# First layer norm in two halves, the attention's constants written during it, and its output in a buffer that is free again

## The chip, the cores and the metric

The kernel runs on one core of one Trainium2 chip. The metric is the device time of one execution in microseconds (us); lower is better. Four compute engines and the DMA queues run their own instruction streams, and semaphores order them against each other.

## The reference, cut to what matters

All tensors are float32, T = 128 x 32 = 4096 tokens of width D = 128. Two stages follow each other, each adding to `x`:

```python
x = x + _L0_ffn_ref(_L0_cond_ref(x, fside, cond), ...)      # Sinkhorn scaling, then a routed FFN
x = x + _L1_ffn_ref(_L1_cond_ref(x, cond, ...), ...)        # a GRU over 32 steps, then the block below
# _L1_ffn_ref:
m = mean(y); v = mean(square(y - m)); n1 = (y - m) * rsqrt(v + 1e-5) * ln1_w + ln1_b
y = y + msa(n1)                     # 16 heads of width 8, 32 tokens of each batch attend to each other
y = y + moe(layernorm(y, ln2_w, ln2_b))     # argmax over 8 experts, gelu, hidden width 512
```

The change touches the first layer norm of `_L1_ffn_ref` and the start of its attention.

## The kernel before, in words

The program is a row of blocks. A block gives every engine a piece of straight code, and the next block begins when all engines have left it. In order: `sinkhorn`, `plan_ffn_gru`, `norm_first`, `attend_and_route`, `experts`. There is no planner: within a block each engine executes its instructions in the order written, and a wait holds everything behind it on that engine.

The GRU leaves its output `ys` with the feature in the partition (`buf_a`). `norm_first` works on N = 32 tiles of 128 tokens, in CHUNKS = 8 chunks of TC = 4 tiles.

- **Turning.** TensorE multiplies each tile of `ys` with `turn_gate` (L864: an identity and eight gate columns), which puts tokens in the partitions. ScalarE copies each chunk from PSUM into `rows` (L894). There are two PSUM buffers `ps_n`.
- **Statistics.** VectorE takes mean and variance of every tile with `bn_stats` (L935), four for each chunk, in a hardware loop. After the eighth chunk it combines them for all 32 tiles at once: seven small operations in `variance` (L809 to L815), each waiting for the one before. ScalarE makes the inverse root by Ln and Exp (L910, L912), and four small operations in `inverse_root` (L820 to L823) refine it.
- **Residual.** Meanwhile TensorE turns the tiles of `x1` (L874) through the same two buffers, and ScalarE copies them out (L899).
- **Leveling and turning back.** VectorE normalises each tile (L944, one instruction a tile, into `ln1_xh`). TensorE turns a chunk back (L885), and ScalarE applies scale and shift and writes `xn_t` (L919).

GpSimd and SyncE have nothing to do in this block.

`attend_and_route` treats the 128 batches in 16 chunks of 8. For a chunk, GpSimd copies the normalised tokens to `xs` (L1082 for the first chunk, L1141 for the others), TensorE projects q and k (L1178, L1179) and v (L1188), ScalarE copies q and writes k once for every head (L1312, L1314) and copies v (L1322), TensorE computes scores (L1201), VectorE takes their maximum and subtracts it (L1385, L1389), ScalarE takes the exponential (L1327), and TensorE turns and mixes (L1215, L1226). GpSimd spreads v over `vb` (L1134).

GpSimd also writes the constants of the block (L1083 to L1121): masks, the identity-like matrices for ranking, tables, and the last columns of `rows`. It is one chain on the semaphore `made`, each step waiting for the one before. TensorE, before its first projection, waits until `made` has reached RANKS = 11:

```python
pe.wait_ge(late.loaded, 16 * late.COUNT)
pe.wait_ge(made, RANKS)
project(0, 0)
```

SyncE waits for `made` too, and then fills the 128 first rows of each expert's part of `sorted_x` in DRAM with one DMA (L1164).

Of the kernel before, what the change touches and what calls it, by code (L numbers as in the profile page):

```python
# [11 lines left out]
P = 128  # L12
# [782 lines left out]
class NormStats:  # L795
# [32 lines left out]
TC = 4  # L828
# [3 lines left out]
def norm_first(nc, io, consts, ys, x1, xn_t, rows, late):  # L832

    ident = consts.ident
    with ExitStack() as ctx:
# [4 lines left out]
        xh = mem.sb("ln1_xh", [P, N, D])  # L840
# [10 lines left out]
        with nc.Block() as block:  # L851

            @block.tensor
            def _(pe):
                mm = nc.tensor.matmul
                pe.wait_ge(gate_in, 1)
# [10 lines left out]
                for c in range(CHUNKS):  # L867
                    if c < 2:
                        pe.wait_ge(y_out, CHUNKS - 1 + c)
                    else:  # L870
                        pe.wait_ge(r_out, c - 1)
                    for k in range(TC):
                        at = (k % 2) * D
                        last = nc.tensor.transpose(ps_n[c % 2][:, k // 2, at:at + D], batches(x1, c * TC + k), ident[:])  # L874
                    last.then_inc(r_mm, 1)
                    if c == 1:
                        pe.wait_ge(g_out, 1)
                        mm(ps_g[:, D:WIDE], proj_t[:], late.turn_gate[:, D:WIDE], start=True, stop=True)
                        mm(ps_g[:, WIDE:WIDE + 8], consts.ones[:], late.gate_shift[:], start=True, stop=True).then_inc(g_mm, 1)
                for c in range(CHUNKS):  # L880
                    pe.wait_ge(xh_done, (c + 1) * TC)
                    if c >= 2:
                        pe.wait_ge(x_out, c - 1)
                    for k in range(TC):
                        last = nc.tensor.transpose(ps_x[c % 2][:, k * B:(k + 1) * B], xh[:, c * TC + k, :], ident[:])  # L885
                    last.then_inc(x_mm, 1)

            @block.scalar
            def _(act):
                nc.scalar.preload_act_table_set("natural_log_exp_and_others")  # L890
                with nc.scalar.Fori(0, CHUNKS // 2) as q:
# [12 lines left out]
                for c in range(3):  # L904
                    residual(c)
# [7 lines left out]
                for c in range(3, CHUNKS):  # L913
                    residual(c)
# [8 lines left out]
            def _(dve):  # L923
# [8 lines left out]
                with nc.vector.Fori(0, CHUNKS) as q:  # L932
                    dve.wait_ge(y_out, q + 1)
                    for k in range(TC):
                        last = v.bn_stats(st.six[:, q * TC + k, :], rows[:, q * TC + k, 0:D])  # L935
# [818 lines left out]
```

## Time and profile before

| | |
|---|---|
| time before, median of 3 runs | 639.91 us (639.65 to 643.46) |
| the profiled execution | 642.09 us, of which its span is 640.1 us |
| busy: TensorE (matmul), VectorE, ScalarE, GpSimd | 515.0, 367.5, 285.4, 137.6 us |
| `norm_first` | from 380.7 to 411.4 us of the span |
| `attend_and_route` | from 411.7 us of the span |

The span runs from the first to the last instruction; 1.99 us of the profiled execution lie around it. In the rows below a duration is that of one instruction or of a run of them (`x4`), and instructions of one engine may overlap by some tens of ns. A bracket tells how long the engine was idle before the row and what released it. PE is TensorE, DVE is VectorE, ACT is ScalarE, POOL is GpSimd, SP is SyncE.

### The profile page before, as it was taken

The numbers are of one execution on the slowest core, as the hardware profiler recorded it, in microseconds if no ns is written. First come the engines' busy times: TensorE is split into PE (matmuls) and PEld (weight loads), VectorE is DVE, ScalarE is ACT, GpSimd is POOL, SyncE is SP. The second block draws the span as 40 slices with busy tenths as digits, with TensorE's granted clock in tenths as the row PEclk, the third lists the DMA queues.
The fourth block names the chain that finished last, engine by engine and source line by source line (L and its number), as shares of the span: only waits on it lengthen the run. The fifth ranks groups of instructions, "written<-read, shape, count | busy, mean of one in ns | idle before, by whom it ended". The sixth has DMA issues, their size and how long they took to land. (4 is left out here: it accounts for less than half of the span.)

```text
span 640.1 us, 35558 instructions
## 1 busy us (share of the span) xinstructions
PE 515.0 (80%) x15366; PEld 419.0 (65%) x15366; DVE 367.5 (57%) x1136; ACT 285.4 (45%) x690; POOL 137.6 (21%) x250
## 2 busy tenths in 40 slices
PE   0888888888878964999999759488888863299995
PEld 0777788777768522666666549366666652299995
DVE  4655555555545622666666535536989997255552
ACT  5222222222214650455555434557757751277772
POOL 2111111111110000000000000253456546145453
PEclk9999999999995695999999999979989995599998
DMA  8060000000000008583321000020011012223330
GB/s 267 10 206 0 0 0 0 0 0 0 0 1 1 0 22 141 113 319 55 78 65 25 1 1 2 1 74 3 1 38 50 35 38 89 88 82 105 110 109 20
DMA packets 22637, 34.37 MB, mean 54 GB/s; under 512 B 3608, under 2 KB 15901, under 8 KB 22200
## 3 DMA queue, kind: packets, MB, share of 16 engines
q1 hardware_dynamic: 19808, 27.23, 16.0%
q0 software_dynamic: 2784, 6.56, 2.9%
q8 instruction: 26, 0.43, 0.3%
q14 instruction: 19, 0.16, 0.1%
HBM read 25.98 MB, written 8.26 MB: 53 GB/s over the span
## 5 line engine op out<-in xcount | busy, mean ns | idle before, releaser
L230 PE MATMUL ps_u<-v_cur,buf_b 128*32 128x32 f32 x7936 | 76.1, 197 | 5.8 <-DVE v_cur L287 1.0
L230 PEld LDWEIGHTS ps_u<-v_cur,buf_b 128*32 128x32 f32 x7936 | 72.5, 109 | 11.1 <-DVE v_cur L287 10.6
L215 PE MATMUL ps_v<-buf_a,u_pad 128*32 128x128 f32 x1984 | 62.3, 279 | 7.3 <-issue 6.0
L564 PE MATMUL ps_y<-act,down 128*128 128x512 f32 x96 | 50.7, 624 | 14.7 <-DVE act L701 14.7
L215 PEld LDWEIGHTS ps_v<-buf_a,u_pad 128*32 128x32 f32 x1984 | 53.7, 112 | 10.9 <-issue 9.2
L554 PE MATMUL ps_h<-buf_c,up 128*128 128x512 f32 x96 | 51.9, 631 | 0.1
L195 ACT ACTIVATE over<-u_diff 128x32 f32<-128x32 f32 x31 | 7.1, 230 | 93.5 <-POOL u_diff L175 93.5
L1564 POOL DMA_INDIRECT out<-yb,token_i x39 | 38.3, 981 | 48.4 <-DVE resid L1666 47.3
L1082 POOL COPY xs<-buf_c 128x256 f32<-128x256 f32 x1 | 0.4, 396 | 222.2 <-POOLq L851 222.2
L179 POOL TENSOR_TENSOR u_hist<-inv_u,r_sum 128x16 f32 x62 | 13.7, 221 | 140.7 <-DVE inv_u L294 140.7
L1587 PE MATMUL m_h<-xT,w_near 128*128 128x128 f32 x312 | 43.1, 283 | 0.0
L1597 PE MATMUL m_y<-w,hid_t 128*128 x312 | 41.4, 276 | 0.1
L1587 PEld LDWEIGHTS m_h<-xT,w_near 128*128 128x128 f32 x312 | 39.6, 199 | 0.2 <-ACT xT L1627 0.2
L1134 POOL TENSOR_TENSOR vb<-vn,row_mask 128x1024 f32<-128x1024 f32 x16 | 30.2, 1890 | 43.5 <-ACT vn L1322 39.3
L282 DVE TENSOR_SCALAR den_v<-ps_v 128x128 f32<-128x128 f32 x62 | 18.0, 291 | 35.5 <-PE ps_v L215 35.5
L1597 PEld LDWEIGHTS m_y<-w,hid_t 128*128 128x128 f32 x312 | 38.2, 193 | 0.3 <-issue 0.3
L1127 POOL DMA_INDIRECT sorted_x<-rows,slot_i x32 | 31.7, 990 | 17.5 <-PE ps_o L1226 9.3
L670 ACT ACTIVATE gate<-ps_gr,gru_b 128x128 f32<-128x128 f32 x32 | 11.7, 364 | 52.5 <-PE ps_gr L613 52.5
L1682 DVE TENSOR_TENSOR yb<-m_y,resid 128x128 f32<-128x128 f32 x39 | 11.4, 292 | 38.8 <-PE m_y L1597 38.8
L287 DVE RECIPROCAL v_cur<-ps_vt 128x64 f32<-128x64 f32 x62 | 33.6, 552 | 0.0
L293 DVE TENSOR_TENSOR den_u<-ps_u,least 128x16 f32<-128x16 f32 x62 | 10.7, 173 | 39.5 <-PE ps_u L230 39.5
L564 PEld LDWEIGHTS ps_y<-act,down 128*128 128x128 f32 x96 | 16.6, 201 | 23.5 <-DVE act L701 16.0
(289 smaller groups left out, 1136.4 us busy)
## 6 DMA issues: line engine op xcount, KB each, us to landing
cw_b<-cw_d SPq DMA_DIRECT2D x16, 512.0 KB, 7.9
xt<-sorted_x SPq DMA_DIRECT2D x39, 136.0 KB, 2.1
w<-in_w SPq DMA_DIRECT2D x2, 2048.0 KB, 16.1
buf_a<-in_x SPq DMA_DIRECT2D x4, 512.0 KB, 6.1
buf_b<-in_x_t SPq DMA_DIRECT2D x4, 512.0 KB, 6.9
buf_d<-in_x_nt SPq DMA_DIRECT2D x1, 2048.0 KB, 10.3
sorted_x<-nobody SPq DMA_DIRECT2D x1, 1088.0 KB, 5.1
out<-yb,token_i POOLq DMA_INDIRECT x39, 2.5
```

The lines of the kernel that those rows point to most:

```text
L179: g.tensor_tensor(u_hist[:, i + 2, gs], inv_u[:, h, :], r_sum[:, gs], ALU.mult).then_inc(u_kept[h], 1)
L215: last = mm(ps_v[h][32 * j:32 * j + 32, 0:D], u_pad[:, h, j, 32 * i4:32 * i4 + 32], K[:, g * D:(g + 1) * D], start=i4 == 0, stop=i4 == TI - 1)
L230: last = mm(rows_u[h][32 * q:32 * q + 32, g, :], KT[:, b * N:(b + 1) * N], v_cur[:, h, k:k + 1].broadcast_to([P, WIDE]), start=True, stop= ...
L282: v.tensor_scalar(den_v[:, h, :], ps_v[h][:, 0:D], EPS, None, ALU.max).then_inc(v_den[h], 1)
L287: v.reciprocal(v_cur[:, h, :], ps_t[h][:, 0:HBT]).then_inc(v_ready[h], 1)
L554: mm(ps_h[p % 2][:], up[:, j * P:(j + 1) * P], pt_n[:, q * W:(q + 1) * W], start=True, stop=True).then_inc(h_mm, 1)
L564: mm(ps_y[q % 2][:], down[:, ORDER[k], :], act2[:, p % SLOTS_H, :], start=k == 0, stop=k == J - 1).then_inc(y_mm, 1)
L1127: g.indirect_dma_start(sorted_x, bass.IndirectOffsetOnAxis(ap=tables.slot_i[:, t:t + 1], axis=0), rows[:, t, :], None).then_inc(tables.sen ...
L1134: g.tensor_tensor(vb[:, k % 2].rearrange("p b j r e -> p (b j) r e")[:, :, :, 0:DK], vn[:, k % 2, :].rearrange("p (a d) -> p a d", d=DK)[: ...
L1564: nc.gpsimd.indirect_dma_start(out, bass.IndirectOffsetOnAxis(ap=token_i[:, d:d + 1], axis=0), yb[:, k, :], None, bounds_check=T - 1, oob_ ...
L1587: last = mm(ps_h[d % 2][:, q * P:(q + 1) * P], w1_near[:, d % NEAR, q * P:(q + 1) * P], x_t[:, d % 2, :], start=True, stop=True)
L1597: last = mm(ps_y[d % 2][:, 0:D], hid_t[:, d % 2, q, :], w2[:, bass.ds(at + q * D, D)], start=q == 0, stop=q == Q - 1)
```

## The change

`norm_first` keeps its work and its instruction counts on TensorE, and changes the order. The 32 tiles are in two halves of 16. VectorE takes the statistics of the first half, combines them and begins to level, and takes the statistics of chunks 5 to 7 between the leveled chunks. The combining is done twice on 16 columns: four chained operations in `variance`, two in `middle`, four in `inverse_root`. The loops of ScalarE and VectorE in this block are written out. The constants and the DMA that fills `sorted_x` are in this block, on GpSimd and SyncE. The leveled tiles go to `buf_b`, which the GRU stage has consumed, and not to a buffer of their own.

```diff
-    def variance(self, v, c):
-
-        s = self.six
-        c.step(v.tensor_tensor(self.mean[:], s[:, :, 1], s[:, :, 4], ALU.add))
-        c.step(v.tensor_tensor(self.a[:], s[:, :, 1], s[:, :, 4], ALU.subtract))
-        c.step(v.tensor_tensor(self.a[:], self.a[:], self.a[:], ALU.mult))
-        c.step(v.tensor_scalar(self.a[:], self.a[:], 0.25, LN_EPS, ALU.mult, ALU.add))
-        c.step(v.tensor_tensor(self.var[:], s[:, :, 2], s[:, :, 5], ALU.add))
-        c.step(v.tensor_scalar(self.mean[:], self.mean[:], 0.5, None, ALU.mult))
-        c.step(v.scalar_tensor_tensor(out=self.var[:], in0=self.var[:], scalar=1.0 / D, in1=self.a[:],
-                                      op0=ALU.mult, op1=ALU.add))
-
-    def inverse_root(self, v, c):
-
-        c.step(v.tensor_tensor(self.a[:], self.rstd[:], self.rstd[:], ALU.mult))
-        c.step(v.tensor_tensor(self.a[:], self.a[:], self.var[:], ALU.mult))
-        c.step(v.tensor_scalar(self.a[:], self.a[:], -0.5, 1.5, ALU.mult, ALU.add))
-        c.step(v.tensor_tensor(self.rstd[:], self.rstd[:], self.a[:], ALU.mult))
+    def variance(self, v, c, ts):
+
+        s, a, mean, var = self.six[:, ts, :], self.a[:, ts], self.mean[:, ts], self.var[:, ts]
+        c.step(v.tensor_tensor(a, s[:, :, 1], s[:, :, 4], ALU.subtract))
+        c.step(v.scalar_tensor_tensor(out=a, in0=a, scalar=0.25, in1=a, op0=ALU.mult, op1=ALU.mult))
+        c.step(v.tensor_tensor(var, s[:, :, 2], s[:, :, 5], ALU.add))
+        c.step(v.scalar_tensor_tensor(out=var, in0=var, scalar=1.0 / D, in1=a, op0=ALU.mult, op1=ALU.add))
+
+    def middle(self, v, c, ts):
+
+        s, mean = self.six[:, ts, :], self.mean[:, ts]
+        c.step(v.tensor_tensor(mean, s[:, :, 1], s[:, :, 4], ALU.add))
+        c.step(v.tensor_scalar(mean, mean, 0.5, None, ALU.mult))
+
+    def inverse_root(self, v, c, ts):
+
+        a, var, rstd = self.a[:, ts], self.var[:, ts], self.rstd[:, ts]
+        c.step(v.tensor_tensor(a, rstd, rstd, ALU.mult))
+        c.step(v.scalar_tensor_tensor(out=a, in0=var, scalar=LN_EPS, in1=a, op0=ALU.add, op1=ALU.mult))
+        c.step(v.tensor_scalar(a, a, -0.5, 1.5, ALU.mult, ALU.add))
+        c.step(v.tensor_tensor(rstd, rstd, a, ALU.mult))
...
+class Setup:
...
+        self.block_mask = mem.sb("block_mask", [P, 4, 4])
...
-def norm_first(nc, io, consts, ys, x1, xn_t, rows, late):
+def norm_first(nc, io, consts, ys, x1, xn_t, xh, rows, late, setup, tables):
 
     ident = consts.ident
+    PARTS = 2
+    TP = N // PARTS
+    CP = CHUNKS // PARTS
...
-        xh = mem.sb("ln1_xh", [P, N, D])
...
+            @block.gpsimd
+            def _(pool):
+                g = nc.gpsimd
+                E, J, R, DK = E_MOE, 4, 4, 8
+                block_mask, row_mask, vb = setup.block_mask, setup.row_mask, setup.vb
+                g.memset(setup.eps[:], LN_EPS).then_inc(setup.eps_in, 1)
+                c = Chain(pool, setup.made)
+                c.step(g.memset(block_mask[:], 1.0))
...
+                for k in range(PACK):
+                    c.step(g.memset(setup.places[:, :, k], float(E ** k)))
+
+            @block.sync
+            def _(sp):
+                sp.wait_ge(setup.made, Setup.FILL - 1)
+                sp.dma_start(tables.sorted_x.rearrange("(e s) w -> s e w", s=CAP)[0:P],
+                             tables.nobody[:, None, :].broadcast_to([P, E_MOE, ROW])).then_inc(tables.filled, 16)
...
+                for c in range(CP):
+                    normed(c)
+                    residual(c)
+                pe.wait_ge(g_out, 1)
+                mm(ps_g[:, D:WIDE], proj_t[:], late.turn_gate[:, D:WIDE], start=True, stop=True)
+                mm(ps_g[:, WIDE:WIDE + 8], consts.ones[:], late.gate_shift[:], start=True, stop=True).then_inc(g_mm, 1)
+                for c in range(CP, CHUNKS):
+                    residual(c)
+                for c in range(CP, CHUNKS):
+                    normed(c)
...
+                def root(part):
+                    ts = slice(part * TP, (part + 1) * TP)
+                    act.wait_ge(stats, part + 1)
+                    nc.scalar.activation(st.root[:, ts], st.var[:, ts], ACT.Ln, bias=setup.eps[:]).then_inc(act_own, 1)
+                    act.wait_ge(act_own, part + 1)
+                    nc.scalar.activation(st.rstd[:, ts], st.root[:, ts], ACT.Exp, scale=-0.5).then_inc(rooted, 1)
...
+                act.wait_ge(setup.eps_in, 1)
+                for c in range(CP + 1):
+                    turned(c)
+                root(0)
+                for c in range(CP + 1, CHUNKS):
+                    turned(c)
...
+                for c in range(CP):
+                    normed(c)
                     residual(c)
+                    if c == 1:
+                        root(1)
...
-                with nc.vector.Fori(0, CHUNKS) as q:
...
+                first, second = slice(0, TP), slice(TP, N)
+                for n in range(CP):
+                    spread(n)
+                dve.wait_ge(own, c.n)
+                st.variance(v, c, first)
+                dve.sem_inc(stats, 1)
+                st.middle(v, c, first)
+                spread(CP)
+                dve.wait_ge(rooted, 1)
+                st.inverse_root(v, c, first)
+                for n in range(CP):
+                    for t in range(n * TC, (n + 1) * TC):
+                        level(t)
+                    if n + 1 < CP:
+                        spread(CP + 1 + n)
+                    if n + 2 == CP:
+                        dve.wait_ge(own, c.n)
+                        st.variance(v, c, second)
+                        dve.sem_inc(stats, 1)
+                        st.middle(v, c, second)
+                dve.wait_ge(rooted, 2)
+                st.inverse_root(v, c, second)
+                for t in range(TP, N):
+                    level(t)
...
-                c = Chain(pool, made)
                 g.tensor_copy(xs[:, 0], xn_t[:, 0:CB, :]).then_inc(x_in, 1)
-                c.step(g.memset(block_mask[:], 1.0))
...
+        tables = Tables(keep, sorted_x)
+        xh = buf_b[:].rearrange("p (t d) -> p t d", d=D)
+        with ExitStack() as until:
+            setup = Setup(Memory(nc, until))
+            norm_first(nc, io, consts, ys, x1, xn_t, xh, rows, late, setup, tables)
+            attend_and_route(nc, io, consts, xn_t, rows, late, setup, tables, sorted_x)
```

VectorE from the first statistics to the last leveled tile, before. `ln_six` holds the raw statistics, `rows` the turned tokens.

```order
L935 BN_STATS ln_six<-rows 128x6
L932 REGISTER_ALU
L932 COMPARE_AND_BRANCH
L809 TENSOR_TENSOR ln_mean<-ln_six 128x32
...
L815 SCALAR_TENSOR_TENSOR ln_var<-ln_var,ln_a 128x32
L820 TENSOR_TENSOR ln_a<-ln_rstd 128x32
...
L944 TENSOR_SCALAR ln_xh<-rows,ln_mean,ln_rstd 128x128 x32
```

The same place in the changed kernel:

```order
L1040 BN_STATS ln_six<-rows 128x6 x16
L809 TENSOR_TENSOR ln_a<-ln_six 128x16
...
L1040 BN_STATS ln_six<-rows 128x6 x4
L823 TENSOR_TENSOR ln_a<-ln_rstd 128x16
...
L1044 TENSOR_SCALAR buf_b<-rows,ln_mean,ln_rstd 128x128 x4
L1040 BN_STATS ln_six<-rows 128x6 x4
...
L1044 TENSOR_SCALAR buf_b<-rows,ln_mean,ln_rstd 128x128 x16
```

Half of the leveling now stands behind 16 statistics and the first combining; the other half stands last.

ScalarE in `norm_first`, after the turned chunks, before:

```order
L903 COPY proj_t<-ps_g 128x128
L899 COPY rows<-ps_n 128x4x128 x3
L907 COPY w_proj<-ps_g 128x8
L908 COPY gate_sums<-ps_g 128x8
L910 ACTIVATE ln_root<-ln_var 128x32
L912 ACTIVATE ln_rstd<-ln_root 128x32
L899 COPY rows<-ps_n 128x4x128 x5
```

The same place in the changed kernel:

```order
L1010 COPY proj_t<-ps_g 128x128
L1000 ACTIVATE buf_c<-ps_x,ln_wb 128x512
L988 COPY rows<-ps_n 128x4x128
L1000 ACTIVATE buf_c<-ps_x,ln_wb 128x512
L988 COPY rows<-ps_n 128x4x128
L994 ACTIVATE ln_root<-ln_var,eps 128x16
L996 ACTIVATE ln_rstd<-ln_root 128x16
L1000 ACTIVATE buf_c<-ps_x,ln_wb 128x512
L988 COPY rows<-ps_n 128x4x128
```

Before, all eight L919 came behind all eight L899; now the first four of each alternate, and the second half's root stands behind the second pair.

GpSimd at the start of `attend_and_route`, before:

```order
L1082 COPY xs<-buf_c 128x256
L1083 MEMSET block_mask 128x16
L1084 AFFINE_SELECT block_mask<-block_mask 128x16
...
L1104 AFFINE_SELECT before<-before 128x128
...
L1121 MEMSET places 128x5 x8
L1141 COPY xs<-buf_c 128x256
```

The same place in the changed kernel:

```order
L925 MEMSET places 128x5 x8
L879 UNCONDITIONAL_BRANCH
L1194 UNCONDITIONAL_BRANCH
L1197 COPY xs<-buf_c 128x256
L1217 COPY xs<-buf_c 128x256
L1210 TENSOR_TENSOR vb<-vn,row_mask 128x128x8
```

The constants end in the block before, and the two copies of the first two chunks follow each other.

## Rows read from the trace of the kernel before

**Rows 1.** The page: the granted TensorE clock in 40 slices of the span, tenths.
```profile
PEclk9999999999995695999999999979989995599998
```

**Rows 2.** Timeline of VectorE in `norm_first`: start us, us, engine, line, operation, count [idle before, releaser].
```profile
390.33 0.98 DVE L935 BATCH_NORM_STATS2 ln_six<-rows  x4 [0.78 <-ACT rows L894]
...
397.37 0.98 DVE L935 BATCH_NORM_STATS2 ln_six<-rows  x4 [0.78 <-ACT rows L894]
...
399.81 0.19 DVE L815 SCALAR_TENSOR_TENSOR ln_var<-ln_var,ln_a 128x32 f32<-128x32 f32 x1
...
400.61 0.19 DVE L820 TENSOR_TENSOR ln_a<-ln_rstd 128x32 f32<-128x32 f32 x1 [0.61 <-ACT ln_rstd L912]
...
401.50 8.30 DVE L944 TENSOR_SCALAR ln_xh<-rows,ln_mean,ln_rstd 128x128 f32<-128x128 f32 x32
```

**Rows 3.** VectorE in the attention: timeline row, then groups (count, busy us, mean ns).
```profile
436.55 0.47 DVE L1410 BATCH_NORM_STATS2 six<-rows 128x6 f32<-128x128 f32 x2
...
L1410 DVE BATCH_NORM_STATS2 six<-rows 128x6 f32<-128x128 f32 x4 | 0.9, 279 | 0.0
```

**Rows 4.** Timeline of ScalarE in `norm_first`: last turned chunk, residual, normed.
```profile
396.51 0.61 ACT L894 COPY rows<-ps_n 128x544 f32 x1 [1.15 <-PE ps_n L864]
...
400.48 1.05 ACT L899 COPY rows<-ps_n 128x512 f32<-128x512 f32 x2
...
403.80 1.49 ACT L919 ACTIVATE buf_c<-ps_x,ln_wb 128x512 f32 x2
...
410.66 0.78 ACT L919 ACTIVATE buf_c<-ps_x,ln_wb 128x512 f32 x1 [0.25 <-PE ps_x L885]
```

**Rows 5.** Timeline of GpSimd at the start of `attend_and_route`: the copy, the eleventh constant, the last.
```profile
411.73 0.40 POOL L1082 COPY xs<-buf_c 128x256 f32<-128x256 f32 x1 [222.20 <-POOLq L851]
...
415.08 0.30 POOL L1104 TENSOR_SCALAR_AFFINE_SELECT before<-before 128x128 bf16<-128x128 bf16 x1
...
418.36 1.26 POOL L1121 MEMSET places<- 128x5 f32 x8
```

**Rows 6.** The page, transfers: the fill of the sorted rows.
```profile
sorted_x<-nobody SPq DMA_DIRECT2D x1, 1088.0 KB, 5.1
```

**Rows 7.** Timeline of TensorE and ScalarE, first two chunks of the attention.
```profile
415.48 1.19 PE L1178 MATMUL ps_qk<-xs,w_qkv 128*128 128x256 f32 x2 [4.97 <-POOL before L1104]
...
417.65 0.37 ACT L1312 COPY qs<-ps_qk 128x256 f32<-128x256 f32 x1 [6.21 <-POOL rows L1113]
...
419.63 1.52 PE L1201 MATMUL ps_ss<-km,qs 32*32 32x128 f32 x64 [1.09 <-ACT km L1314]
...
421.08 1.22 PE L1178 MATMUL ps_qk<-xs,w_qkv 128*128 128x256 f32 x2
...
423.19 0.37 ACT L1312 COPY qs<-ps_qk 128x256 f32<-128x256 f32 x1 [3.44 <-PE ps_qk L1179]
...
425.18 1.06 PE L1201 MATMUL ps_ss<-km,qs 32*32 32x128 f32 x64 [1.05 <-ACT km L1314]
```

**Rows 8.** The same timeline, third chunk: project, heads, scores.
```profile
427.23 0.60 PE L1178 MATMUL ps_qk<-xs,w_qkv 128*128 128x256 f32 x2
...
428.30 0.37 ACT L1312 COPY qs<-ps_qk 128x256 f32<-128x256 f32 x1 [0.23 <-PE ps_qk L1179]
...
430.49 1.06 PE L1201 MATMUL ps_ss<-km,qs 32*32 32x128 f32 x64 [0.28 <-ACT km L1314]
```

**Rows 9.** Stretches: from:to, length, busy and (count) by engine, PEclk, DMA share, GB/s.
```profile
413.00:414.00 1.00, 0.00 (x0) 0.00 (x0) 0.00 (x0) 0.00 (x0) 0.81 (x4) 0.85 0.03 8
423.00:424.00 1.00, 1.00 (x65) 0.92 (x64) 0.74 (x1) 0.81 (x3) 0.00 (x0) 0.53 0.00 0
```

**Rows 10.** Timeline of GpSimd and VectorE, the first `moments` of the attention.
```profile
443.33 1.89 POOL L1134 TENSOR_TENSOR vb<-vn,row_mask 128x1024 f32<-128x1024 f32 x1 [5.17 <-ACT vn L1322]
...
444.46 0.78 DVE L1416 TENSOR_TENSOR gap<-six 128x4 f32<-128x4 f32 x1
```

**Rows 11.** Timeline of TensorE in the fourth chunk: the rest of its scores.
```profile
438.48 0.49 PE L1201 MATMUL ps_ss<-km,qs 32*32 32x128 f32 x26 [1.81 <-issue]
```

More of the change, by code:

```diff
@@ L855, in _, with residual, normed @@
                 mm = nc.tensor.matmul
+                def residual(c):
+                    if c < 2:
+                        pe.wait_ge(y_out, CHUNKS - 1 + c)
+                    else:
+                        pe.wait_ge(r_out, c - 1)
+                    for k in range(TC):
+                        at = (k % 2) * D
+                        last = nc.tensor.transpose(ps_n[c % 2][:, k // 2, at:at + D], batches(x1, c * TC + k), ident[:])
+                    last.then_inc(r_mm, 1)
+                def normed(c):
+                    pe.wait_ge(xh_done, (c + 1) * TC)
+                    if c >= 2:
+                        pe.wait_ge(x_out, c - 1)
+                    for k in range(TC):
+                        last = nc.tensor.transpose(ps_x[c % 2][:, k * B:(k + 1) * B], xh[:, c * TC + k, :], ident[:])
+                    last.then_inc(x_mm, 1)
                 pe.wait_ge(gate_in, 1)
@@ L890, in _, with turned @@
                 nc.scalar.preload_act_table_set("natural_log_exp_and_others")
-                with nc.scalar.Fori(0, CHUNKS // 2) as q:
-                    for k in range(2):
-                        act.wait_ge(y_mm, q * 2 + k + 1)
-                        nc.scalar.copy(rows[:, bass.ds((q * 2 + k) * TC, TC), 0:WIDE].rearrange("p (h t) w -> p h t w", h=2),
-                                       ps_n[k][:, :, 0:2 * WIDE].rearrange("p h (t w) -> p h t w", w=WIDE)).then_inc(y_out, 1)
+                def turned(c):
+                    act.wait_ge(y_mm, c + 1)
+                    nc.scalar.copy(rows[:, c * TC:(c + 1) * TC, 0:WIDE].rearrange("p (h t) w -> p h t w", h=2),
+                                   ps_n[c % 2][:, :, 0:2 * WIDE].rearrange("p h (t w) -> p h t w", w=WIDE)).then_inc(y_out, 1)
                 def residual(c):
@@ L958, with __init__ @@
 class Tables:
-    def __init__(self, mem):
+    def __init__(self, mem, sorted_x):
+        self.sorted_x = sorted_x
         self.slot_i = mem.sb("slot_i", [P, G], I32)
@@ L979, in __init__, with attend_and_route @@
         self.last = [f + k - 1 for f, k in zip(self.first, self.SIZES)]
-def attend_and_route(nc, io, consts, xn_t, rows, late, tables, sorted_x):
+def attend_and_route(nc, io, consts, xn_t, rows, late, setup, tables, sorted_x):
     ident, ones = consts.ident, consts.ones
@@ L1103, in _ @@
-                c.step(g.memset(before[:], 1.0))
-                c.step(g.affine_select(out=before[:], in_=before[:], compare_op=ALU.is_ge, fill=0.0, base=-1,
-                                       pattern=[[1, P]], channel_multiplier=-1))
-                c.step(g.memset(tables.nobody[:], 0.0))
-                c.step(g.memset(tables.nobody[:, TOKEN:TOKEN + 1], float(T)))
-                c.step(g.memset(rows[:, :, TOKEN + 1:ROW], 0.0))
-                c.step(g.iota(rows[:, :, TOKEN], pattern=[[N, G]], base=0, channel_multiplier=1,
-                              allow_small_or_imprecise_dtypes=True))
@@ L1111, in _ @@
-                for q in range(BG):
-                    c.step(g.memset(ahead[q * N:(q + 1) * N, :], float(q * (G * N - N))))
-                c.step(g.tensor_scalar(rows[:, :, TOKEN], rows[:, :, TOKEN], ahead[:, 0:1], None, ALU.add))
-                c.step(g.iota(lane[:], pattern=[[0, 1]], base=0, channel_multiplier=1,
-                              allow_small_or_imprecise_dtypes=True))
-                c.step(g.iota(tile_no[:], pattern=[[1, TABLE]], base=0, channel_multiplier=0,
-                              allow_small_or_imprecise_dtypes=True))
@@ L1118, in _ @@
-                c.step(g.iota(tile_at[:], pattern=[[P, TABLE]], base=P, channel_multiplier=0,
-                              allow_small_or_imprecise_dtypes=True))
-                for k in range(PACK):
-                    c.step(g.memset(places[:, :, k], float(E ** k)))
                 def send(t):
```

167 lines of the change are left out of this document (77 added, 90 removed).

## The prediction

> **What bounds the kernel now.** I read the page first. The stages follow each other, and no engine is busy in all of them, so the question is what ends each part of the stage that the change touches. The clock line has 16 us a slice; between the long stretches at full clock stands one slice at 7, from 416 to 432 us, where the attention begins [rows 1].
>
> In `norm_first` I went along VectorE. Up to the eighth chunk it waits for TensorE and ScalarE: four statistics take 0.98, and it idles 0.78 before each group. Behind the eighth group, at 398.35, comes a chain with nothing beside it on VectorE: seven steps to 400.00 (0.236 each), the root on ScalarE (0.61), four steps to 401.50 (0.89), and 32 leveled tiles in 8.30 (0.26 each, 1.04 a chunk), ending at 409.80 [rows 2]. ScalarE follows at VectorE's pace and ends at 411.44, 1.64 later [rows 4].
>
> Then the attention. GpSimd copies the first chunk from 411.73 to 412.13, but TensorE starts only at 415.48, after 4.97 idle, released by the eleventh constant, which ends at 415.38 [rows 5, 7]. Its clock fell to half in the stretch from 413 to 414 (0.85 is 0.7 us at full clock, so at 413.7, 3.2 us after the last matmul), and came back at the very end of the stretch from 423 to 424 [rows 9]. The first two chunks run at half clock.
>
> **The change, part by part.**
>
> *1. The statistics in halves.* The eighth group can't start earlier than before, but when it comes half of the leveling is partly done. VectorE from the fourth group, which ends at 391.31 [rows 2]: four steps of combining 0.94, two of `middle` 0.47, then chunk 4's statistics. Outside a loop two statistics take 0.47 and one 0.28, so one follows the other after 0.19 and four take 0.76 [rows 3]. Then the inverse root, 0.89; then three chunks leveled (3.12) with three groups of statistics (2.28) between them; then the second combining, 0.94. The sum is 391.31 + 0.94 + 0.47 + 0.76 + 0.89 + 3.12 + 2.28 + 0.94 = 400.7. The 16 columns instead of 32 I count as nothing gained: a step is mostly its fixed time. The last turned chunk leaves ScalarE at 397.12 [rows 4], before VectorE asks for it at about 399, so all inputs are there.
>
> *2. ScalarE is late next.* VectorE alone would go on with 0.47, 1.04, 0.89 and 16 tiles (4.15) to 407.3, and with the old tail of 1.64 the block would end at 408.9. But ScalarE has the second half's root behind two normed and two residual chunks. It finishes those by about 400.2 (397.12, 0.3 for `proj_t`, 2 x (0.75 + 0.53), and one hand-over) and waits there for 400.7; everything behind it waits as well, and TensorE's third to eighth residual wait for its copies. From 400.7 it has: the root 0.6; six residual copies at 0.53 (1.05 for two), 3.2; six normed at 0.75 (1.49 for two), 4.5 [rows 2, 4]; two copies of 8 columns, which I estimate at half a root, 0.3; and about four hand-overs to TensorE and back at 0.25 each [rows 4], 1.0. That is 9.6, an end at 410.3 instead of 411.44: **1.1 us** gained. Bounds: with the loop's 0.98 for each group 0.9 less, 0.2; with no hand-over in sight 2.1.
>
> *3. The constants.* GpSimd's chain of constants took from 412.13 to 419.62, 7.5 us [rows 5]; now it runs from 380.8 to about 388.5, where GpSimd did nothing. It covers itself: the only waiters in the block are ScalarE's first wait for `eps`, one short memset behind which its table load lies anyway, and SyncE. The attention starts with the copy (0.29 after the block's end, 0.40 long), and TensorE about 0.1 after it: 0.8 instead of 4.04 (415.48 - 411.44). **3.25 us** gained. The copy for the second chunk follows at once, instead of at 419.7; it was not waited for. Bounds: nothing, if another wait ends as late; 3.25.
>
> *4. The clock.* With this, TensorE's pause is from some 0.9 before the block's end to 0.8 after it, 1.7 to 2 us, and it fell only after 3.2 before. So I take full clock for the first two chunks. From the first projection to the scores of the second chunk it was 9.70: projection 2.17, ScalarE to scores 1.98, scores 1.45, projection 2.11, ScalarE to scores 1.99 [rows 7]. At full clock the third chunk shows 1.07 for the projection and 1.06 for the scores [rows 8]: 1.07 + 1.98 + 1.06 + 1.07 + 1.99 = 7.17. VectorE's maximum and difference fit in behind ScalarE. **2.5 us** gained. Bounds: 0 and 2.5.
>
> *5. The fill of `sorted_x`* (1088 KB, 5.1 to landing [rows 6]) moves from 416 to about 385, beside the turned chunks, which use no DMA. `buf_b` costs nothing: it is the same write into SBUF. Behind the second chunk all engines have the order they had, so the gain is carried to the end. Both: 0.
>
> The rule against part 3 is about a port. In this trace a VectorE sum of 4 columns with two inputs from SBUF took 0.78 us, from 444.46 to 445.24, and GpSimd's long multiply ended at 445.22 [rows 10]. GPSIMD Engine Reference (the Trainium skill, section Specifications) says the SBUF interfaces are shared with VectorE, with contention when a VectorE instruction has two SBUF inputs. The row agrees. By the page's rule taken alone, with every constant beside VectorE, it would be the second rival below and 634.9. Here the constants end at about 388.5 and the first such instruction of the combining comes at 391.3, so I charge nothing.
>
> **The sum.** 1.1 + 3.25 + 2.5 = 6.85. The profiled execution took 642.09 with a span of 640.1; by the sum it becomes 635.2, its span 633.2. It lies 2.2 above the median of the three runs, 639.91, and the difference belongs to the run, not to the stage. The median becomes **633.1**.
>
> **Rivals.**
>
> *The clock falls all the same* (0.15). For it: the new block has a pause of some 2 us on TensorE while ScalarE waits for the second root, and the pause at the attention follows. Against it: both are shorter than 3.2. Part 4 goes: 635.6.
>
> *GpSimd holds VectorE up* (0.07). If the two slow each other on the port and the constants last beyond 391.3, each of the first half's two-input steps waits up to the length of a constant's instruction; three at up to 0.59 (0.78 in [rows 10] against 0.19 in [rows 2]) are 1.8, and all of it lands on ScalarE's root: 634.9.
>
> *Something else ends as late as the constants did* (0.05). Part 3 goes, part 4 half: 637.6. Against it: the trace names the constants and the other inputs are older.
>
> *Code arrives late* (0.13, slower than before in 0.05). TensorE stood 1.81 us in the middle of 64 equal matmuls with nothing to wait for [rows 11]. If that is code that has not arrived, the written-out loops of VectorE and ScalarE move where their streams reach new code, and a less idle TensorE has less pause to hide it in. Each such stall on the leading engine is 1.81: one gives 634.9, two 636.7, three 638.5; from the fourth on the kernel is slower than before, 640.3, and with five 642.1. Against many: TensorE's count of instructions is unchanged.
>
> Runtime: NRT & Kernel Launch (the Trainium skill, section Instruction fetch mechanics) says that instructions are fetched in blocks ahead of their use, mostly hidden, and that a taken branch to a block not held costs a stall. By that the written-out loops would cost little; no row here shows which engine's code was late.
>
> **How the numbers follow.** My forecast has 0.55 and its own range of 631.2 to 635.0 (part 2 between its bounds, part 4 partly there, and half a us for the rest). 0.05 is left for a better result than that, for instance the 1.81 of the fourth chunk falling away. The range goes to 638 to take in the clock, the port, two stalls and the lost part 3, and starts at 631: what lies outside is under 2 in 10. A measurement of this kernel can tell about 1%, 6.4 us, from no change; that is 633.5, close to my forecast. Some three fifths of the forecast's own chance and the better cases lie below it, 0.40; I say faster 0.43, within 1% 0.52, slower 0.05.
>
> **What would show it.** Right: the first projection within 1 us of the last normed copy; PEclk full from there; first to second scores as in [rows 8]; `norm_first` ending about 1 us sooner, with ScalarE waiting about 0.5 before the second Ln. Wrong: a wait of TensorE at the attention's start that names anything but the copy; a clock dip there; two-input VectorE rows above 0.3 before 393; idle rows of 1.8 released by issue. The forecast fails most easily in part 4, which rests on one fall of the clock seen once.

## The result and the profile after

In six runs each, the changed kernel took 634.96 us in the median against 641.66; the ratio is 0.9892, with a 95% interval of 0.9844 to 0.9941. A second series, in the same rounds as two experiments, gave 635.46 against 643.80, 0.9883 (0.9831 to 0.9935). A ratio comes from the single runs and not from the two medians, and one slow run of one kernel (experiment 3) is left out of its ratio. The gain is 1.1%, and the interval (0.6 to 1.6%) doesn't tell whether it is more than the 1% that I had set as a border. The median that I had forecast, 633.1, was 6.8 below a median of 639.91 from three runs; with three more the median before is 641.66, and 634.96 lies 6.7 below that. The profiled execution took 634.63 with a span of 632.8; I had said 635.2 and 633.2.

The runs of before scatter over 8 us, and the stages ahead of the change begin `norm_first` between 379.0 and 382.1 us of the span. So I compare stretches of the traces, from the first VectorE instruction of `norm_first` (`turn_gate<-ident`) to the first scores of the attention's second chunk:

| us | `norm_first` | its end to the first projection | to the second chunk's scores | sum |
|---|---|---|---|---|
| before | 30.69 | 4.04 | 9.70 | 44.43 |
| predicted | 29.6 | 0.8 | 7.2 | 37.6 |
| changed | 29.80 | 0.82 | 7.35 | 37.97 |
| gained | 0.89 | 3.22 | 2.35 | 6.46 |

The stages ahead of it were 0.51 shorter in this trace, and what follows the second scores was 0.38 shorter: 6.46 + 0.51 + 0.38 = 7.35, and the spans differ by 7.3. The last two numbers are within what such stretches differ by from one trace to the next. `norm_first` itself differs by 0.2: VectorE's first wait for TensorE in it is 0.48 in some traces and 0.64 to 0.69 in the others, those in which the clock fell to half before the block or within its first 0.7 us, and these blocks are 0.18 to 0.27 longer for the same kernel (changed 29.80 against 30.04 and 30.07). Before and changed have 0.48 each, so their 0.89 compares like with like.

VectorE in `norm_first`, the timeline of the changed kernel (columns as in [rows 2]): ScalarE's fourth turned chunk and VectorE's fourth group, a leveled chunk, the statistics behind it, the next leveled chunk, the last 16 tiles.

```profile
388.86 0.61 ACT L983 COPY rows<-ps_n 128x544 f32<-128x544 f32 x1 [1.15 <-PE ps_n L963]
389.51 0.87 DVE L1040 BATCH_NORM_STATS2 ln_six<-rows 128x6 f32<-128x128 f32 x4 [0.89 <-ACT rows L983]
...
393.43 1.12 DVE L1044 TENSOR_SCALAR buf_b<-rows,ln_mean,ln_rstd 128x128 f32<-128x128 f32 x4
...
394.46 0.87 DVE L1040 BATCH_NORM_STATS2 ln_six<-rows 128x6 f32<-128x128 f32 x4
395.24 1.10 DVE L1044 TENSOR_SCALAR buf_b<-rows,ln_mean,ln_rstd 128x128 f32<-128x128 f32 x4
...
402.22 4.20 DVE L1044 TENSOR_SCALAR buf_b<-rows,ln_mean,ln_rstd 128x128 f32<-128x128 f32 x16
```

Against [rows 2], the tiles of the first half begin at 393.43 and lie between the last statistics, and after the second root 16 tiles are left and not 32. A group of four outside the loop leads to the next instruction after 0.78 (394.46 to 395.24), 0.76 being the figure I took from [rows 3]. A group also starts sooner behind ScalarE's copy: in the loops 0.25 after its end (396.51 + 0.61 = 397.12 in [rows 4], 397.37 in [rows 2]), written out 0.04 (389.47, 389.51). Counted from the stage's start the fourth group comes at 9.27 instead of 9.58.

ScalarE in the same stretch, which answers to [rows 4]: the second Ln, the fourth normed chunk, three residual rows behind it, the last four normed chunks.

```profile
399.87 0.31 ACT L994 ACTIVATE ln_root<-ln_var,eps 128x16 f32<-128x16 f32 x1 [0.87 <-DVEq L1065]
...
402.22 0.78 ACT L1000 ACTIVATE buf_c<-ps_x,ln_wb 128x512 f32<-128x512 f32 x1 [0.65 <-PE ps_x L952]
...
404.00 0.59 ACT L988 COPY rows<-ps_n 128x512 f32<-128x512 f32 x1 [0.40 <-PE ps_n L944]
404.86 0.59 ACT L988 COPY rows<-ps_n 128x512 f32<-128x512 f32 x1 [0.27 <-PE ps_n L944]
405.80 1.30 ACT L988 COPY rows<-ps_n 128x512 f32<-128x512 f32 x2 [0.35 <-PE ps_n L944]
407.00 3.04 ACT L1000 ACTIVATE buf_c<-ps_x,ln_wb 128x512 f32<-128x512 f32 x4
```

ScalarE waited 0.87 for the second variance. Behind it ScalarE waits four times more, 0.65 + 0.40 + 0.27 + 0.35 = 1.67, and its last four normed chunks run without a gap, 3.04 for four. VectorE had ended at 406.42, so ScalarE sets the block's end of 410.04. The 0.65 is TensorE's pause, handed on. The three idle times of 0.27 to 0.40 are waits for TensorE, whose clock was at half just then. The granted clock in stretches of 1 us (columns as in [rows 9]), and the TensorE row that ends its pause:

```profile
402.00:403.00 1.00, 1.00 (x11) 1.00 (x10) 0.96 (x5) 0.78 (x2) 0.00 (x0) 0.90 0.00 0
403.00:404.00 1.00, 1.00 (x7) 1.00 (x7) 1.00 (x5) 0.61 (x3) 0.00 (x0) 0.50 0.00 0
406.00:407.00 1.00, 1.00 (x10) 1.00 (x9) 0.42 (x2) 0.87 (x2) 0.00 (x0) 0.90 0.00 0
411.00:412.00 1.00, 1.00 (x15) 0.62 (x19) 0.00 (x0) 0.00 (x0) 0.06 (x1) 1.00 0.00 0
```

```profile
401.52 0.66 PE L952 MATMUL ps_x<-ident,buf_b 128*128 128x128 f32 x4 [2.24 <-DVE buf_b L1044]
```

TensorE stood from 399.29 to 401.52, 2.24 us, for tiles that VectorE had put behind the second combining. At 402.8 (0.90 in its stretch), when it had been busy again for 1.3 us, its clock fell to half until 406.2. At the attention's start the clock is full.

The start of the attention, which answers to [rows 5, 7]:

```profile
410.32 0.40 POOL L1197 COPY xs<-buf_c 128x256 f32<-128x256 f32 x1 [22.58 <-SPq L1192]
...
410.86 0.67 PE L1248 MATMUL ps_qk<-xs,w_qkv 128*128 128x256 f32 x2 [1.64 <-POOL xs L1197]
...
412.08 0.37 ACT L1382 COPY qs<-ps_qk 128x256 f32<-128x256 f32 x1 [2.04 <-PE ps_qk L1249]
...
414.07 1.06 PE L1271 MATMUL ps_ss<-km,qs 32*32 32x128 f32 x64 [1.41 <-ACT km L1384]
...
416.22 0.37 ACT L1382 COPY qs<-ps_qk 128x256 f32<-128x256 f32 x1 [2.04 <-PE ps_qk L1249]
...
418.21 1.06 PE L1271 MATMUL ps_ss<-km,qs 32*32 32x128 f32 x64 [1.33 <-ACT km L1384]
```

TensorE is released by the copy and not by the constants. The two stretches from ScalarE's copy of q to the scores are 1.99 each as before. The scores take 1.06 as in [rows 8]; from projection to ScalarE it is 1.22 and 1.16, where [rows 8] had 1.07.

### The profile page after: what moved, and what is told of

It is laid out like the page before. It is cut to its first block and busy times, and to the rows that moved or that the text cites. A ratio compares the mean times of both kernels' runs of the same rounds, so it can differ in the third digit from the quotient of the medians.

```text
span 632.8 us, 35435 instructions
## 1 busy us (share of the span) xinstructions
PE 513.4 (81%) x15366; PEld 419.5 (66%) x15366; DVE 362.8 (57%) x1145; ACT 285.8 (45%) x692; POOL 138.5 (22%) x250
## 5 line engine op out<-in xcount | busy, mean ns | idle before, releaser
L202 ACT COPY v_hist<-v_cur 128x64 f32 x62 | 15.2, 245 | 37.8 <-DVE v_cur L287 37.8
```

The source lines that it names most:

```text
L202: nc.scalar.copy(v_hist[:, i + 1, h * HBT:(h + 1) * HBT], v_cur[:, h, :]).then_inc(v_kept[h], 1)
```

## The experiments

**1 and 2. One part alone.** The first is the changed kernel with the layer norm of before, on TensorE, ScalarE and VectorE. The diffs are against the changed kernel, where nothing else is said.

```diff
-                for c in range(CP):
-                    normed(c)
-                    residual(c)
...
+                for c in range(CHUNKS):
+                    pe.wait_ge(xh_done, (c + 1) * TC)
...
-                st.variance(v, c, first)
...
+                st.variance(v, c)
```

> The constants and the fill run in norm_first as in the change, but the layer norm is the one of before: one piece, loops, all statistics before the root. Theory (three terms add up: halves 0.9, constants 3.2, clock 2.35 us): norm_first lasts about 31.0 us from the last GRU step as before, TensorE starts the attention 0.8 us after it, and the first two chunks take 7.35 us, so the kernel is 5.6 us faster than before. Rival (the halves carry the gain, the constants were only one of several late inputs): less than 2 us. Rival (the clock falls without the halves): the first two chunks take 9.7 us and the gain is 3.2 us.

The second has the layer norm in halves and the constants at the attention's start.

```diff
                 g.tensor_copy(xs[:, 0], xn_t[:, 0:CB, :]).then_inc(x_in, 1)
+                c = Chain(pool, setup.made)
+                c.step(g.memset(block_mask[:], 1.0))
...
```

> The layer norm in two halves as in the change, but the constants (all but the eps value) and the fill are back at the start of the attention. Theory: norm_first is 0.9 us shorter, TensorE starts 4.0 us after its end at half clock and the first two chunks take 9.7 us: 0.9 us faster than before in sum. Rival (two halves and the written-out loops bring more than the trace of norm_first shows, for example by where code is fetched later): 2 us or more. Rival (GpSimd's constants beside the statistics cost something in the changed kernel): norm_first is shorter here than in the changed kernel, by more than 0.3 us.

| | time | ratio to before | norm | to projection | to scores | sum |
|---|---|---|---|---|---|---|
| constants alone | 635.82 | 0.9897 (0.9853 to 0.9941) | 30.70 | 0.81 | 9.35 | 40.86 |
| halves alone | 639.78 | 0.9974 (0.9947 to 1.0) | 29.78 | 3.89 | 9.69 | 43.36 |

The halves alone give 0.91 us in `norm_first`, as in the changed kernel; its length of 29.78 beside 29.80 (first wait 0.48 in both) also shows that the constants beside the statistics cost nothing there. In times this share can't be told: the interval of the halves reaches 1.0, and the constants alone have the changed kernel's ratio within the noise. "Halves" here holds the loops written out too; no run has one without the other, and 0.31 us of the 0.91 came before the first combining (9.27 against 9.58 above). The constants alone give the 3.23 of the wait. Their third column was a surprise: 9.35, at half clock, though TensorE's pause was 1.75 and not 4.97. First projection and second scores of that trace, and the clock:

```profile
410.67 0.84 PE L1200 MATMUL ps_qk<-xs,w_qkv 128*128 128x256 f32 x2 [1.75 <-POOL xs L1149]
...
420.02 1.06 PE L1223 MATMUL ps_ss<-km,qs 32*32 32x128 f32 x64 [1.33 <-ACT km L1336]
```

```profile
410.00:411.00 1.00, 0.33 (x2) 0.33 (x3) 0.46 (x3) 0.00 (x0) 0.74 (x2) 1.00 0.00 0
411.00:412.00 1.00, 1.00 (x4) 0.56 (x2) 0.00 (x0) 0.00 (x0) 0.00 (x0) 0.52 0.00 0
```

The fall comes at 411.0 (0.52 in the stretch from 411), 2.1 us after the last matmul of `norm_first` and 0.4 us after the next had begun. This kernel's ratio is nevertheless that of the changed kernel (0.9897, 0.9892), so the trace may not be typical.

**3. The clock by itself.** If the third term is TensorE's clock, matmuls that nobody reads must bring it in the kernel before, with the constants where they were (this diff is against the kernel before).

```diff
+                for _ in range(16):
+                    mm(ps_o[:, 0:P], ident[:], ident[:], start=True, stop=True)
                 pe.wait_ge(made, RANKS)
```

> The kernel before, and 16 matmuls of 128x128 whose result nobody reads are put on TensorE between the block's start and its wait for the constants. TensorE still starts the attention when the eleventh constant is there, 4.0 us after norm_first. If the third term is the clock, it stays full, the first two chunks take 7.35 us instead of 9.7, and the kernel is 2.35 us faster than before. Rival (the first two chunks were slow for another reason: the fill's transfers beside them, or GpSimd's constants beside them): they still take 9.7 us at full clock and the time is that of before.

The time was 638.05, ratio 0.9939 (0.9908 to 0.9970). TensorE's timeline and clock (a row counts each of the 16 matmuls twice):

```profile
410.21 5.44 PE L1282 MATMUL ps_o<-ident 128*128 128x128 f32 x32 [1.23 <-PEq L851]
...
415.48 0.60 PE L1178 MATMUL ps_qk<-xs,w_qkv 128*128 128x256 f32 x2
...
422.76 1.06 PE L1201 MATMUL ps_ss<-km,qs 32*32 32x128 f32 x64 [1.33 <-ACT km L1316]
```

```profile
410.00:411.00 1.00, 0.79 (x4) 0.82 (x5) 0.00 (x0) 0.00 (x0) 0.68 (x3) 0.68 0.00 0
413.00:414.00 1.00, 1.00 (x7) 1.00 (x7) 0.07 (x1) 0.00 (x0) 0.81 (x6) 0.61 0.00 0
415.00:416.00 1.00, 1.00 (x9) 0.95 (x9) 0.00 (x0) 0.00 (x0) 0.69 (x5) 1.00 0.67 218
```

From the first projection to the second scores it takes 7.28 with the fill and the constants still beside it, which refutes the rival: TensorE at full clock is enough. But my 16 matmuls were too many: the clock fell at 410.4, just after they had begun, was back only at 413.8, and they delayed the projection to 5.58 after the block's end. From the stage's start to the second scores this trace gained only 0.67 (43.76 against 44.43), and the ratio says 1.9 to 5.9 us; where the rest comes from isn't shown. So I repeated it with 8.

> The kernel before with 8 unread matmuls in TensorE's wait for the constants. With 16 they ended 1.5 us after the constants and delayed the first projection. 8 end before the constants do, so TensorE starts 4.0 us after norm_first as before, and if the clock term is right the first two chunks take 7.35 us and the kernel is 2.35 us faster than before. Rival (8 are too few to bring the clock back up before the first projection): the first two chunks take 8.4 to 9.7 us and the gain is under 1.3 us.

The timeline of that kernel, projection and scores of both chunks, and GpSimd's copy for the second:

```profile
414.19 0.70 PE L1178 MATMUL ps_qk<-xs,w_qkv 128*128 128x256 f32 x2 [1.67 <-POOL before L1104]
...
417.43 1.06 PE L1201 MATMUL ps_ss<-km,qs 32*32 32x128 f32 x64 [1.41 <-ACT km L1316]
418.44 0.40 POOL L1141 COPY xs<-buf_c 128x256 f32<-128x256 f32 x1
...
418.89 0.70 PE L1178 MATMUL ps_qk<-xs,w_qkv 128*128 128x256 f32 x2 [0.41 <-POOL xs L1141]
...
422.05 1.06 PE L1201 MATMUL ps_ss<-km,qs 32*32 32x128 f32 x64 [1.33 <-ACT km L1316]
```

The time was 641.85 against 643.80, ratio 0.9960 (0.9924 to 0.9995). The projection starts 4.00 after the block and the clock is full all through, but the stretch to the second scores took 7.86, neither of the two figures that I had named: the first chunk ran as at full clock (414.19 to 417.43), the second took 4.62 to its scores instead of 4.14. The row of the second projection names the cause: TensorE idled 0.41 for GpSimd's copy of the second chunk, which stands behind all constants and ended at 418.84. At half clock nobody waited for that copy, as the prediction says; at full clock it is late. With 16 matmuls the projection came so late itself that the copy was there. So the clock alone is worth 1.84 here (9.70 - 7.86), and the other 0.5 of the third column needs the full clock and the constants out of the way. Behind the second scores this trace is 5.2 us longer than that of before (220.1 against 214.9), for a reason that isn't shown.

**4. Does the order of work decide where the clock falls?** The changed kernel and the one with the constants alone were profiled once more, unchanged.

> The changed kernel once more, for a second look at its clock. In its first trace the clock fell at 402.8 us, in the middle of norm_first, after TensorE's pause of 2.24 us, and stayed full at the start of the attention. If the order of work decides that, this trace shows the same again and the first two chunks take 7.35 us. If it is chance, the fall can come at the attention's start instead and they take about 9.3 us.

> The kernel with the constants alone moved, for a second look. In its first trace the clock fell 2.1 us after the last matmul of norm_first although TensorE had begun the attention again, and the first two chunks took 9.35 us. If the order of work decides that (a second half of norm_first with TensorE at two thirds busy, then a pause of 1.75 us), it falls here again. If it is chance, it can stay full here and the two chunks take 7.35 us.

In the changed kernel it was the same: a fall in the middle of `norm_first`, at 404.7, after a pause of 2.25, full at the attention's start, 30.07 + 0.83 + 7.34 = 38.24. A third trace (below) gave a fall at 405.2 and 38.21. The constants alone were not the same: the pause was 1.75 again, the clock stayed full through it, and the stretch took 7.35; in sum 39.10, 5.3 less than before, where I had expected 5.6 of this kernel. Its timeline, first projection and second scores:

```profile
412.46 0.67 PE L1200 MATMUL ps_qk<-xs,w_qkv 128*128 128x256 f32 x2 [1.75 <-POOL xs L1149]
...
419.81 1.06 PE L1223 MATMUL ps_ss<-km,qs 32*32 32x128 f32 x64 [1.33 <-ACT km L1336]
```

So a pause of 1.75 us was followed by a fall in one trace and not in the other. The changed kernel has its fall earlier each time, during the residual copies, and then none at the attention. The two other kernels with this order (the halves alone, and experiment 5) fall in `norm_first` at the same place, 3.5 and 3.8 us after that pause began; with the halves alone, whose pause at the attention is 4.71, a second fall comes there.

**5. Constants beside the combining.** My argument that the constants cost nothing was that they end first. Here they do not.

```diff
                 c = Chain(pool, setup.made)
+                pool.wait_ge(y_out, 3)
```

> The changed kernel, but GpSimd starts its constants only when the third chunk is turned, so that they run beside VectorE's first combining and not ahead of it. Theory of the prediction (they cost nothing because they end before the combining): now VectorE's operations with two inputs from SBUF are held, each by up to 0.6 us, the first inverse root comes up to 1.8 us later, and norm_first ends by 0.5 to 1.8 us later than in the changed kernel. Rival (constants this short don't hold VectorE): its seven combining steps stay at 0.22 us each and norm_first ends within 0.2 us of the changed kernel.

GpSimd's first constant and three of VectorE's steps in the timeline of that kernel:

```profile
388.10 0.11 POOL L889 MEMSET block_mask<- 128x16 f32 x1 [7.71 <-ACT rows L984]
...
390.75 0.19 DVE L809 TENSOR_TENSOR ln_a<-ln_six 128x16 f32<-128x16 f32 x1
...
391.94 0.25 DVE L818 TENSOR_SCALAR ln_mean<-ln_mean 128x16 f32<-128x16 f32 x1
...
393.21 0.25 DVE L824 SCALAR_TENSOR_TENSOR ln_a<-ln_var,ln_a 128x16 f32<-128x16 f32 x1
```

Most operations with two SBUF inputs (L809, L811 and others) keep their 0.16 to 0.19; two steps show 0.25 instead of 0.17, L824 with two such inputs and L818 with one. From the fourth group to the second Ln it took 10.51 instead of 10.36, and `norm_first` 30.17, against 30.04 and 30.07 in the two traces of the changed kernel with the same first wait. The rival holds: these constants don't hold VectorE by more than 0.15 us in all. The time was 634.12, ratio 0.9888 (0.9847 to 0.9929), as the changed kernel's. The hold of [rows 10] stands beside a GpSimd instruction of 1.89 us; none of the constants takes longer than 0.66, and most of them only write. Whether the length or the kind of instruction makes the difference isn't shown.

**6. Another order.** The changed kernel's own rows name what is left: 0.87 of ScalarE before the second Ln, and 2.24 of TensorE.

```diff
-                for c in range(CP):              # scalar; tensor alike, without the root
+                for c in range(2):
                     normed(c)
                     residual(c)
-                    if c == 1:
-                        root(1)
+                normed(2)
+                root(1)
+                residual(2)
+                residual(3)
...
                 for c in range(CP, CHUNKS):
                     residual(c)
-                for c in range(CP, CHUNKS):
-                    normed(c)
+                    normed(c - 1)
+                normed(CHUNKS - 1)
```

> The changed kernel with another order on ScalarE and TensorE in norm_first: ScalarE takes the second root behind the third normed chunk instead of behind the second pair, and residual and normed chunks alternate to the end, with two residual chunks before the fourth normed one. In the changed kernel ScalarE waited 0.87 us for the second variance, TensorE idled 2.24 us and its clock then fell to half for 3.4 us. Theory (ScalarE's order sets the end of norm_first): it ends 1.2 to 2.0 us earlier than in the changed kernel, near VectorE's last tile plus 1.6 us, with no dip of the clock at its second half; the kernel is 1.2 to 2.0 us faster than the changed one. Rival (VectorE sets the end): less than 0.4 us. Rival (the clock dip comes all the same): about 1 us.

The timeline of that kernel: the second Ln, TensorE after its two longest pauses, the last normed chunks, the first projection.

```profile
399.13 0.31 ACT L997 ACTIVATE ln_root<-ln_var,eps 128x16 f32<-128x16 f32 x1 [0.19 <-DVEq L1070]
...
400.21 0.71 PE L944 MATMUL ps_n<-ident,x 128*128 128x128 f32 x4 [0.84 <-ACT rows L991]
...
402.64 0.66 PE L952 MATMUL ps_x<-ident,buf_b 128*128 128x128 f32 x4 [0.75 <-DVE buf_b L1049]
...
405.62 1.57 ACT L1003 ACTIVATE buf_c<-ps_x,ln_wb 128x512 f32<-128x512 f32 x2
...
408.01 0.67 PE L1253 MATMUL ps_qk<-xs,w_qkv 128*128 128x256 f32 x2 [1.64 <-POOL xs L1202]
```

ScalarE's wait before the Ln is 0.19. TensorE's pauses are 0.84 and 0.75, and the clock is full from 386.8 to the end of the block and on. `norm_first` takes 27.91, 2.1 less than in the two traces of the changed kernel with the same first wait; VectorE ends at 405.66, and the block 1.53 behind it. Sum 27.91 + 0.82 + 7.34 = 36.07. The time was 631.81, ratio 0.9847 (0.9809 to 0.9886). Then both side by side, in the same rounds:

> The changed kernel, timed on the same chip and in the same rounds as the next two. 6.5 to 7 us faster than before, ratio 0.989 to 0.990; the clock falls in the middle of norm_first and not at the attention's start, as in its two traces so far.

> The order without gaps again, beside the changed kernel. By its first trace norm_first is 1.9 us shorter, so 1.9 us faster than the changed kernel, ratio to before 0.986 to 0.987. Rival (the gain is given back where the attention's fourth chunk waits for code): within 0.5 us of the changed kernel.

| | time | ratio to before | norm | to projection | to scores | sum |
|---|---|---|---|---|---|---|
| changed | 635.46 | 0.9883 (0.9831 to 0.9935) | 30.04 | 0.82 | 7.35 | 38.21 |
| other order | 633.23 | 0.9852 (0.9807 to 0.9897) | 27.73 | 0.82 | 8.93 | 37.48 |

The intervals overlap, the medians differ by 2.2 us, and the stage itself by 2.3 (27.73 has the short first wait and 30.04 the long one; against 29.80 it is 2.1 again). In this trace of the other order the clock fell 0.8 us into the attention, at 408.6, after a pause of 1.64, and took back 1.6 us of it (stretches of that trace, columns as in [rows 9]):

```profile
408.00:409.00 1.00, 1.00 (x4) 0.44 (x3) 0.00 (x0) 0.00 (x0) 0.00 (x0) 0.79 0.00 0
409.00:410.00 1.00, 1.00 (x65) 0.95 (x64) 0.00 (x0) 0.81 (x3) 0.00 (x0) 0.50 0.00 0
```

**7. The copies early.** In the same order, GpSimd makes the first two chunks' copies within `norm_first`.

```diff
+                pool.wait_ge(x_out, 1)
+                for k in range(2):
+                    g.tensor_copy(setup.xs[:, k], xn_t[:, k * 8:(k + 1) * 8, :]).then_inc(setup.x_in, 1)
...
-                g.tensor_copy(xs[:, 0], xn_t[:, 0:CB, :]).then_inc(x_in, 1)
...
-                chunk_in(1)
```

> The kernel with the order without gaps, and GpSimd's copies of the first two chunks of the attention are made inside norm_first, behind the first normed chunk that they read. Theory: TensorE starts the attention 0.2 to 0.3 us after the block's end instead of 0.82, the clock stays full, so 0.5 to 0.6 us faster than the order without gaps and 2.4 us faster than the changed kernel. Rival (TensorE's start waits for its own code or for the end of the block, not for the copy): no difference. Rival (the copies beside VectorE hold its second combining up): norm_first ends up to 0.4 us later and nothing is gained.

The timeline of that kernel: a chunk of levels, the copies beside it, the first projection.

```profile
396.40 1.28 DVE L1054 TENSOR_SCALAR buf_b<-rows,ln_mean,ln_rstd 128x128 f32<-128x128 f32 x4
...
396.86 0.74 POOL L930 COPY xs<-buf_c 128x256 f32<-128x256 f32 x2 [10.01 <-ACT buf_c L1008]
...
407.98 0.67 PE L1256 MATMUL ps_qk<-xs,w_qkv 128*128 128x256 f32 x2 [1.30 <-PEq L881]
```

The time was 630.34, ratio 0.9852 (0.9822 to 0.9882): the least median of all, but no other ratio than experiment 6. TensorE starts 0.48 after the block's end instead of 0.82 and is released by the block's end itself, so a third of a us and not half was to be had; and `norm_first` takes 28.14, 0.23 longer, with a chunk of levels beside the copies at 1.28 instead of 1.09 (396.30 in the timeline of experiment 6). Both rivals hold in part, and the sum (35.97 against 36.07) is no gain that can be told.

## Why the prediction was right

**Part 1, the halves on VectorE.** Right: from the fourth group's start to the second Ln I had 10.37 (400.7 - 390.33), and it took 10.36. What I had at nothing is that loops written out bring the groups themselves earlier: the fourth came 0.31 earlier in the stage, and with it the Ln, at 399.87 and not at 400.2 (my 400.7 less the 0.51 of the stages ahead). ScalarE therefore waited 0.87 for it, where I had said about 0.5, having finished earlier as well.

**Part 2, ScalarE late next.** Right in kind: it waits for the second root and then sets the end. The size was 0.89 for 1.1, and that is nearer than the working deserved, because two misses cancel in part. From the Ln to the end I had 9.6 and it took 10.17; the term that was too small is the hand-overs, 1.67 where I had 1.0. Against these 0.57 stand the 0.31 above. I had not seen that TensorE's pause, which I named only in a rival, would make ScalarE wait 0.65 for a normed chunk and would cost TensorE its clock for 3.4 us while ScalarE waits for its turned chunks. That the loss is in the order is shown by experiment 6; how much of it is the clock is not shown.

**Part 3, the constants.** Right: 3.22 for 3.25, alone (experiment 1) and together. Nothing else came as late; GpSimd's constants ended at 387.7, and even beside the combining they cost 0.15 at most (experiment 5). GPSIMD Engine Reference (the Trainium skill, section Specifications) has contention where a VectorE instruction has two SBUF inputs. By experiment 5 these constants bear little of that out: 0.08 more for one instruction with two inputs and as much for one with one input, and nothing for the others; [rows 10] remain as its case.

**Part 4, the clock.** The forecast came true, 2.35 for 2.5, and experiment 3 shows that 1.84 of it is the clock by itself; the rest came only because part 3 also brought the second chunk's copy forward, a wait that the full clock would otherwise have laid bare. My reason for it did not hold: I argued that a pause shorter than 3.2 us keeps the clock. Where the clock had been full through the second half of `norm_first`, a pause of 1.23 to 1.75 was followed by a fall in three of seven traces: constants alone one of two, the other order one of two, copies early none of one, unread matmuls one of two. In the changed kernel it was full at the attention in three of three, and in experiment 5 too; each time it had fallen and come back just before. That this is the reason is not shown. So that the forecast met the number owes something to luck: I gave the rival "the clock falls all the same" 0.15 at 2.5 us, three of seven comparable pauses brought a fall, and in the two traces where it came at the attention without more matmuls it cost 2.0 and 1.6. Here it came in the block before.

**Part 5.** The fill cost nothing that a row shows; TensorE was busy at 1.00 in every stretch beside it.

**Code that arrives late.** TensorE's stall in the fourth chunk stayed, 1.28 for 1.81. Whether it is code at all was not tried.

The sum was 6.85 predicted and 6.46 in the stage; the profiled execution came out 0.6 below my 635.2 only because 0.9 was gained outside the stage. By the ratios the runs say 6.9 and 7.5, with intervals of some 3 us to either side, so what speaks for the single terms is the traces.

## What to carry to other kernels

When a chain of small steps closes a stage, halving the data hides one half's chain behind the other half's work; then look at which engine now waits with finished work behind the wait, since of what `norm_first` gave in these runs the larger part lay in ScalarE's and TensorE's order (2.1 us on top of the 0.9 of the halves; the order without the halves was not tried). Constants belong where their engine is idle, ahead of the stage that asks for them, and the first place to look is the row whose releaser is a memset or a select. A clock term of a few us should be priced as a chance, not as a sum. And when an engine gets faster, ask which inputs were on time only because it was slow: the second chunk's copy was one.

## What the runs showed that I had not expected

TensorE's clock often fell when the pause was already over. The fall came 3.5 to 3.8 us after the pause began and 1.3 to 1.5 us after it ended in the changed kernel (pause of 2.24, in three traces of three), 2.1 us after the pause began with the constants alone, 2.4 with the other order, 1.4 with the 16 matmuls. In the kernel before it came 3.2 us after the pause began, with the pause still on. A pause of 0.84 and one of 0.75 close together (experiment 6) brought none. Unread matmuls at the right place are no free remedy: 16 of them ran into half clock and were late by 1.5 us.
